# A DiT block with self and cross attention on one core: order of the first loads and of the modulation product, place of two fills and a load, and order of the last maxima on VectorE

## The reference, cut to what matters

```python
c_proj = silu(c) @ W_mod + b_mod                       # (32, 768)
shift_a, scale_a, gate_a, shift_m, scale_m, gate_m = split(c_proj, 6)
q, k, v = split((ln(x) * (1 + scale_a) + shift_a) @ W_qkv + b_qkv, 3)
x = x + gate_a * (softmax(q k^T / sqrt(8)) v @ W_proj + b_proj)
k_c, v_c = split(ln(context) @ W_kvc + b_kvc, 2)
x = x + softmax((ln(x) @ W_qc + b_qc) k_c^T / sqrt(8)) v_c @ W_cproj + b_cproj
h = gelu((ln(x) * (1 + scale_m) + shift_m) @ W_mlp1 + b_mlp1) @ W_mlp2 + b_mlp2
x = x + gate_m * h
```

## Time and profile before

| what | value |
|---|---|
| median of 3 runs | 376.72 us (376.64 to 378.62) |
| the profiled execution, its own time | 376.17 us |
| its span | 374.2 us |
| mean granted TensorE clock | 0.968 |
| TensorE, VectorE, ScalarE, GpSimd busy | 91%, 71%, 72%, 56% of the span |

### The profile page before, as it was taken

How to read it: one execution, slowest core, us unless ns; L and a number is a source line. 1 busy time by engine, 2 the same in 40 slices (tenths; PEclk the granted TensorE clock), 3 DMA queues, 4 the chain that set the end, 5 groups by cost and what they waited for, 6 DMA issues and landing times. The chain is left out here.

```text
span 374.2 us, 16029 instructions
## 1 busy us (share of the span) xinstructions
PE 338.9 (91%) x5888; PEld 231.2 (62%) x5888; DVE 264.0 (71%) x671; ACT 269.7 (72%) x526; POOL 210.0 (56%) x479
## 2 busy tenths in 40 slices
PE   4578778999899999999999999998888799999996
PEld 3455545677676777767777676776655355554444
DVE  6965768787788889788888888987866824443401
ACT  2336565888888788887888888887775746776673
POOL 6862677777778677787777778667374300112100
PEclk9955999999999999999999999999999989999999
DMA  5744464434344344434434444344243100101111
GB/s 131 158 102 134 123 149 99 104 92 114 91 104 114 86 100 98 113 90 113 101 72 110 104 100 114 86 102 102 65 102 88 45 3 3 30 28 56 28 28 56
DMA packets 65788, 33.13 MB, mean 89 GB/s; under 512 B 8471, under 2 KB 65495, under 8 KB 65751
## 3 DMA queue, kind: packets, MB, share of 16 engines
q1 hardware_dynamic: 63847, 32.36, 35.6%
q10 hardware_dynamic: 1904, 0.27, 0.6%
HBM read 4.83 MB, written 2.10 MB: 19 GB/s over the span
## 5 line engine op out<-in xcount | busy, mean ns | idle before, releaser
L862 DVE TENSOR_REDUCE mx<-wide 128x8 f32<-128x1024 f32 x64 | 78.2, 1222 | 23.7 <-PE wide L1345 23.3
L1078 ACT ACTIVATE p_c<-wide 128x1024 f32<-128x1024 f32 x64 | 65.5, 1024 | 24.8 <-PE wide L1356 23.8
L1078 ACT ACTIVATE p_s<-wide 128x1024 f32<-128x1024 f32 x64 | 65.6, 1026 | 10.5 <-PE wide L1356 10.5
L862 DVE TENSOR_REDUCE mxc<-wide 128x8 f32<-128x616 f32 x64 | 50.8, 793 | 6.5 <-PE wide L1345 6.2
L1367 PE MATMUL ps_o<-p_s,v_m 128*32 128x128 f32 x1024 | 42.6, 285 | 0.2
L1367 PE MATMUL ps_o<-p_c,vc_m 128*32 128x128 f32 x1024 | 42.2, 283 | 0.1
L1345 PE MATMUL wide<-qk_st 62*128 62x128 bf16 x512 | 26.5, 226 | 9.2 <-DVE mx L862 4.6
L1345 PEld LDWEIGHTS wide<-qk_st 62*128 62x128 bf16 x512 | 15.2, 97 | 25.1 <-DVE mx L862 13.1
L1408 PE MATMUL wide<-m_nT,w_sb 128*128 128x512 f32 x64 | 30.2, 602 | 0.2 <-DVE mxc L862 0.2
L1367 PEld LDWEIGHTS ps_o<-p_s,v_m 128*32 128x32 f32 x1024 | 25.0, 111 | 7.6 <-issue 2.1
L1367 PEld LDWEIGHTS ps_o<-p_c,vc_m 128*32 128x32 f32 x1024 | 24.6, 110 | 6.8 <-issue 0.5
(11 more groups left out here) (182 smaller groups left out, 812.9 us busy)
## 6 DMA issues: line engine op xcount, KB each, us to landing
qk_st<-qkp SPq DMA_DIRECT2D x94, 128.0 KB, 2.5
qkc_st<-qkcp SPq DMA_DIRECT2D x90, 128.0 KB, 2.5
out<-m_out SPq DMA_DIRECT2D x7, 256.0 KB, 2.3
xs<-x SPq DMA_DIRECT2D x3, 512.0 KB, 4.8
qk_st<-nmT SPq DMA_DIRECT2D x64, 4.0 KB
qkc_st<-nmcT SPq DMA_DIRECT2D x64, 4.0 KB
ctx_sb<-ctx SPq DMA_DIRECT2D x3, 308.0 KB
w_sb<-L_xcond_W_mlp SPq DMA_DIRECT2D x2, 256.0 KB, 3.1
```

The costliest lines, as they stand in the source:

```text
L862: nc.vector.reduce_max(mxt[:, b].rearrange("q (x r) -> q r x", r=2)[:, r], src, AX.X, negate=True).then_inc(sems[done], 1)
L1078: nc.scalar.activation(dst[u % 2][:].rearrange("k x q -> k (x q)"), ps_st[:].rearrange("k s x -> k (s x)"), ACT.Exp, scale=SCALE).then_inc ...
```

## The change

The order of several lists changes, and no arithmetic does. SP loads the first piece of x ahead of the modulation weight, and the third piece (`load_x(2)`, 512 KB) only after the first stack has landed. TensorE multiplies the modulation in three parts: (0, 1) at the start, (2, 3) after the transposes of pair 0, (4, 5) after the v rows of pair 0. VectorE makes the tables 0 and 1 and `head_columns` behind the normalisation of pair 0, and the tables 2 to 5 behind `first_keys`. GpSimd does its fills in slot 0 instead of slot -1. The first four of the eight groups of gate rows are spread at the end of slot -1, ahead of the first scores, and the other four in beats 0 and 1 of slot 0. In the drain VectorE modulates the MLP rows of group 1 and takes the maxima of the last pair ahead of the moments and the normalisation of group 2. TensorE transposes group 1 ahead of the fourth chunk of `m_up(0)`, and GpSimd's `split_max(p15, 0)` goes ahead of `m_rstd_step(2)`.

```diff
             sp.dma_start(cond_sb[:], cond).then_inc(sems["cond_in"], 16)
+            load_x(0)
             sp.dma_start(wmod_sb[:], w_mod).then_inc(sems["wm_in"], 16)
-            load_x(0)
...
-            load_x(2)
...
                 if s == -1:
                     w(sp, "qk_in0", 16 * NCMB)
                     load_c(1)
+                    load_x(2)
...
-                if a and a.first():
+                if h and h.first():
                     pool.wait_ge(sems["wc_in"], 16 * 2)
...
+            split_max(p15, 0, mxc, nmc, "mxc_set", "nmch_set", "nmc_set", "mtc_ps")
             m_rstd_step(2)
-            for b in range(G):
-                split_max(p15, b, mxc, nmc, "mxc_set", "nmch_set", "nmc_set", "mtc_ps")
+            split_max(p15, 1, mxc, nmc, "mxc_set", "nmch_set", "nmc_set", "mtc_ps")
...
             def gate_rows(second):
 
+                normalise("x", second, x_of(second), "xt_ps")
+                first_keys()
+                tables(range(2, 6), 2)
                 dve.wait_ge(sems["mod_set"], 2)
                 nc.vector.tensor_copy(gsrc[:, 0:B], mod[:, 2])
-                normalise("x", second, x_of(second), "xt_ps")
-                first_keys()
...
                     if t == 0 and far:
-                        if far.first():
-                            tables(range(2), 1)
-                            head_columns()
...
                         if far.first():
-                            tables(range(2, 6), 2)
+                            tables(range(2), 1)
+                            head_columns()
...
             m_normalise(1, 1)
+            m_modulate(1, 1)
+            cross_maxima(p15, [0])
+            residual(p13, "projc_ps", "proj_c", "x2_set")
+            cross_maxima(p15, [1])
             w(dve, "x2_set", 6)
             m_moments(2)
-            m_modulate(1, 1)
+            cross_maxima(p15, [2, 3])
             m_normalise(2, 0)
-            residual(p13, "projc_ps", "proj_c", "x2_set")
-            cross_maxima(p15, range(NU))
...
-                    if t < NU and h and h.first():
+                    if t < 2 and h and h.first():
                         for n in range(2):
-                            spread(2 * t + n, ps_st[:, n])
+                            spread(2 * t + n + 4, ps_st[:, n])
...
                     biased(a.shift(1))
+                    for n in range(4):
+                        spread(n, ps_st[:, n % 2])
...
+            def modulation(ks):
+                for k in ks:
+                    last = mm(ps_max[:, int(k < 2), k * B:(k + 1) * B], wmod_sb[:, k * C:(k + 1) * C], siluT[:],
+                              start=True, stop=True)
+                    if k in (1, 5):
+                        last.then_inc(sems["mod_ps"], 1)
+
+            modulation((0, 1))
...
                         rows_v()
+                        if a.first():
+                            modulation((4, 5))
...
                         transposed(bank(s, "x_t"), "x", far, T, "xt_ps", GT)
+                        if far.first():
+                            modulation((2, 3))
...
                         tr(rows[0:3, 3 * C:4 * C], g3[:, :, 2 * B], ident16[:]).then_inc(sems["g_ps"], 1)
+                        for n in range(4):
+                            spread(n, ps_st[:, n % 2])
...
-            m_up(0, 0, True, [3])
             after("q_c", p15, 2)
             m_transpose(1, 1, True)
+            m_up(0, 0, True, [3])
             cross_proj(after("obc_t", p13, 1), p13)
```

More of the change, by code:

```diff
@@ L1324, in _ @@
             pe.wait_ge(sems["wm_in"], 16)
-            for k in range(6):
-                last = mm(ps_max[:, int(k < 2), k * B:(k + 1) * B], wmod_sb[:, k * C:(k + 1) * C], siluT[:], start=True, stop=True)
-                if k in (1, 5):
-                    last.then_inc(sems["mod_ps"], 1)
+            def modulation(ks):
[5 more added lines that the diff above has]
+            modulation((0, 1))
             def bank(s, name):
@@ L1605, in slot @@
                         flip_out(bank(s, "obc_t"), "c", e, "oc_set", "obct_ps")
-                    if h and h.first() and t < NU:
+                    if h and h.first() and t < 2:
                         for n in range(2):
-                            spread(2 * t + n, ps_st[:, n])
+                            spread(2 * t + n + 4, ps_st[:, n])
                     if t == 4 and a and a.first():
```

## The result

| what | before | after |
|---|---|---|
| first timing, 4 runs each: median | 377.67 us (376.64 to 378.77) | 381.23 us (379.57 to 384.88) |
| second timing: median | 378.65 us (29 runs, 375.42 to 383.64) | 380.06 us (12 runs, 377.09 to 384.76) |
| the profiled execution, its span | 374.2 us | 379.4 us |

A forecast was written before the change was run, and what follows sets the result against it. TensorE, busy 91% of the span, was taken as the bound, behind a beginning of small dependent steps. Beginning +0.5 and drain -2.05 gave -1.55 us, 374.6 or 375.2 by base; forecast 374.8 us, range 373.2 to 377.0.

The forecast's parts named there:

- the q and k rows 1.1 us earlier: Beginning: with x loaded first and modulation products split, pair 0's rows start at about 8.25 instead of 9.38.
- the moved fills at nothing: Slot 0: GpSimd's fills and column sorts fall where it was idle and cost nothing.
- The late table: Beginning: whole modulation table set at 14.2 instead of 8.6; TensorE stands until then, everything queued behind 2.1 us later.
- The drain: Drain: the last pair's maxima come earlier, TensorE's 1.70 us hole shrinks and the clock stays up: 2.05 us earlier.
- The base: Whole kernel: starting time of the sum, 376.17 us from the profiled execution, against a median of 376.72.
- hide under the transposes: Beginning: tables 0 and 1, the column sort and products (2, 3), 0.9 us, hide under transposes and ScalarE's `modulated`.
- a fill's 1.1 us: Slot 0: possible cost if GpSimd blocks VectorE without the cover, 2.26 us of idle ahead of the maxima.
- The beginning as a whole: Everything up to slot 0's exponentials: entered as +0.5 us, with bounds -0.7 and +1.5.
- (2): Drain: the clock falls all the same in the 1.1 us of holes left, giving 375.6 us; chance 0.18.
- (3): Drain: gains nothing, the 1.70 us hole only moves to waits for ScalarE, giving 376.7 us; chance 0.05.
- rival (4): Beginning: low clock lasts longer as TensorE stands idle more before slot 0; slower, 379 us; chance 0.09.
- Rival (1): Beginning: gains, as the stack ends last; first scores 0.3 us earlier, exponentials 0.7, giving 373.4 us; chance 0.16.

The follow-up runs named there:

- the kernel with the fills that wait: The changed kernel, but GpSimd starts its fills in slot 0 only when VectorE has normalised the context; ratio to before 1.0011.

## Why the prediction was wrong

Two terms of the sum failed: the q and k rows 1.1 us earlier, which came 0.2 us earlier or not at all, and the moved fills at nothing, which cost 0.6 to 2.1 us. The late table was right as a mechanism and came 0.9 to 1.2 us later still. The drain was right.

**The base.** The sum was made against 376.17, and the forecast was set between that and 376.72. Before is 377.67 to 378.70 in the later timings. A profiled execution near the fastest of its kernel, and a median of three, gave no warning of the 8 us between the lowest and the highest of 29.

**"The q and k rows of pair 0 start at about 8.25: 1.1 us earlier"** failed. The load did land as thought (4.41; forecast 4.1), and the transposes ended 0.96 us earlier than before, at 7.52. What failed is the overlap with ScalarE, whose list the forecast took as free. It issues bias loads until 8.23, and `modulated` can't start ahead of that: it started at 8.34, where 8.52 was before. The other profiles show the same. With transposes that end anywhere between 7.10 and 8.17, `modulated` starts at 8.33 to 8.41 in seven of them, 0.11 us behind the last of these issues, and where the issues run to 8.44 (early spreads alone) it starts at 8.55. The second profile of before, without the early load, has the rows at 9.19. So the early x gained nothing there in any kernel, and this term of 1.1 us was worth 0.2 against one profile of before and nothing against the other. With it ScalarE's share for `first_keys` was ready at 12.15 and not at 11.2: hence `first_keys` at 12.28 instead of 11.4 and the table at 15.1 instead of 14.2.

The column sort that would "hide under the transposes" was mis-sized as well, but it mattered less. It took 1.83 us instead of 0.57 (the same four instructions), beside GpSimd's fill of `qkc_st` (L704), which the same normalised rows release, and ended 0.1 us ahead of `modulated`. In the second run of after it took 2.51 us, TensorE waited for it, and the rows came at 9.47, some 0.25 us later by the sort. No kernel here took that fill away, so that it is the fill which holds the sort is read from the traces and not tried.

**"The whole table is set at 14.2 and TensorE stands until then"** was right as a mechanism, and its chain held to the end in after's profile: bias products at 15.15 after a hole of 2.44 us (2.3 forecast), ScalarE's copies at 16.16 (16.5), rows of pair 1 at 17.05 (16.6) at the slow price, 1.19 us at a granted clock of 0.50 in 16 to 18, gate transposes at 19.02 (18.6), and 3.34 us later the first scores (3.2 forecast), with no wait for the stack. The forecast had 20.95 or 21.8; the two runs have 22.36 and 23.27, 0.6 and 1.5 later than the second. The table is 0.9 and 1.2 us later than forecast. From the bias products to the rows of pair 1 it then took 1.90 us in the first run (2.4 forecast), which gave 0.5 back, and 2.53 in the second, where the two bias products took 0.59 and 0.56 us instead of 0.38 and 0.36. The 0.40 us at the first exponentials was given back, as forecast.

**"The moved fills I cost at nothing"** failed. The prediction named the normalisation of the context and its meeting with the column copies, and let it come 0.3 us late. It took 2.83 us longer (3.43 against 0.60). It is not its reader in slot 1 that counts but what stands behind it in VectorE's own list: two fills, the statistics of x and the maxima of slot 0. So it used up the 2.26 us of cover; that list stood 0.5 us later besides, as it follows the first scores (+1.9) and not the exponentials. The maxima came 1.0 us later than the shift of +1.4 alone would have them, TensorE waited 1.72 us for them, and the clock went below full speed again in 40 to 44 us. The meeting is worth the 0.6 to 2.1 us above. The rest of the beginning missed by 1.3 us in the kernel with the fills that wait (+1.8 against the +0.5 entered). Which of the two errors is the larger the timings don't tell. The bound "a fill's 1.1 us" was of the wrong event: it isn't a fill that blocks there. By the rule of the Trainium skill (SBUF — State Buffer, Who interferes with whom) one engine waits for one instruction of the other, which would be a column copy of about 0.26 us; the runs show both engines held together for over 3 us. The measurement decides.

**The beginning as a whole** was entered with +0.5 and a bound of +1.5. It measured +3.8 and +3.2 by slot 1. Modulation alone +4.1, fills alone +1.8, spreads alone +1.6 and the loads -0.6 don't add up, because they share waits: without the modulation the loads, the spreads and the waiting fills give -1.7 together. The price of the split modulation, with the late table and the late column sort that it brings, can be read by difference: +1.8 with it and the waiting fills, -1.7 without it, 3.5 us, of which some 0.4 is the clock; by the timings it is 4.0. How much of it is TensorE's wait for the table alone isn't shown.

**The drain** was right: -2.05 forecast; 2.3 to 2.6 measured in nine profiles. The hole went, the new wait for ScalarE is 0.33 us (0.35 forecast), the next scores came 1.23 us after the first (1.25 forecast), the clock stayed up. Of the 2.05 the forecast put 1.0 on the clock, and the second profile of before has just that. The chain of TensorE's pieces was 0.4 us shorter than I made it, 9.82 instead of 10.2. Rivals (2) and (3) are out.

**The rivals.** The sign is that of rival (4), slower. Its mechanism, a longer low clock, is a part of it: in after's profile half speed lasts to 36.4 us instead of 37.4, but comes back from 39.8 to 43.2. It comes right behind the wait of 1.72 us for the maxima, but that this wait is its cause isn't shown: in the second execution of after TensorE waits 1.64 us at the same place, and the granted clock is 1.00 in 40 to 44. Two bounds of that rival don't follow from its rows. 5.81 us of work in 8 at 1.8 times its length lose at most 0.24 us for each us of low clock, not 0.45, and 3.45 us at 0.1 take 35 us of it, not 30. Rival (1), a beginning that gains, is right for the loads: the kernels without the split modulation do that.

**Still open.** Why an issue of SP takes 1.8 us instead of 0.6 in slots 2 and 3 of most executions, and a stack copy of slot 1 lands late in some, wasn't tried. Nor was it settled whether that explains the 1.0118 of the first four runs against the 1.0034 of the twelve. No kernel moved ScalarE's bias loads behind `modulated`, which would show what the early x is worth. What VectorE and GpSimd contend for in slot 0 is not shown either, only that starting them one behind the other ends it.

## What to carry to other kernels

A load that lands earlier is worth only what the other engines' lists let through: follow each of them, DMA issues too, up to the instruction that needs it. When an instruction is moved, ask not only what it waits for but what it releases on the other engines and what will lie beside it there; a cost of nothing is only as good as that list. A wait for a whole table in an in-order queue delays everything queued behind it, so split the product only if what reads the last part is late too. And take a part of a bundle by itself: here loads, fills, spreads and drain won 0.95%, and one further edit, the split modulation, took it all away again (ratio 1.0011).

## What the runs showed of the hardware

- A VectorE `tensor_scalar` (77x128, fp32) and GpSimd copies (128x64, fp32) that meet hold each other: 3.43 and 3.36 us together, 0.60 and 0.52 apart. It came with the same lengths in each of the three profiles in which they meet (after twice, fills alone).
- A VectorE `tensor_scalar` of 32 columns stayed held through four GpSimd fills in a row, 4.00 and 3.59 us. VectorE's own fills, which lie beside GpSimd's in slot 0, took 0.91 us each.
- ScalarE's own DMA issues take its time: three of 0.50 to 0.68 us, back to back up to 8.23, held an activation whose input was ready at 7.52 until 8.34.
- The granted clock on record doesn't show every slow stretch near the start. In the second run of after it is 1.00 from 22 to 36 us, but eight score products take 0.61 us there, as at a clock of 0.50 in after, and 0.40 at 40.42. The lengths of like instructions are the better witness.
- Repeated executions of one kernel on one core lie up to 8 us apart (375.42 to 383.64 in 29 runs), and the clock falls at differing places in the profiled ones. All but one of the intervals here are 0.3 to 0.4% to either side, so differences under that could be read, if at all, only from shifts inside the traces.
